# Attention in a fused layer: the exp over three PSUM banks instead of two, and one continuous score pipeline over all head pairs

## The reference

```python
xn = _layernorm(x)
# q, k, v: each holo_linear(xn, basis, phase, amp), split into 16 heads of 64
attn = jnp.einsum('bhqd,bhkd->bhqk', q, k) * scale      # scale = 64 ** -0.5
attn = jax.nn.softmax(attn, axis=-1)
out = jnp.einsum('bhqk,bhkd->bhqd', attn, v)
# out -> holo_linear(..., basis_o, phase_o, amp_o)
x = x + attention(xn) + ffn(xn)                         # ffn: 8 experts + shared MLP
```

## Time and profile before

| what | us |
|---|---|
| runs | 3964.14 and 4123.48, median 4043.81 |
| profiled execution | 3966.25 |
| its span on the slowest core (core 7) | 3964.7 |
| spans of the 8 cores | 3949.5 to 3964.7 |
| first exp of attention starts | 505.5 |
| last exp of attention starts | 1259.5 |
| exps: 512, together busy | 571.8 |

### The profile page before, as it was taken

The page is one execution under the profiler, slowest core; times in us unless marked ns, Lnnn a source line. Parts: engine busy times, 40 slices in busy tenths (PEclk is TensorE's granted clock), DMA queues, the critical chain, the costliest instruction groups (busy, mean ns, idle before and its releaser), DMA issues.

```text
span 3964.7 us, 46389 instructions; the slowest of 8 cores (3949.5 to 3964.7 us)
## 1 busy us (share of the span) xinstructions
PE 3153.2 (80%) x13795; PEld 1235.1 (31%) x13795; DVE 1567.0 (40%) x2502; ACT 939.1 (24%) x1201; POOL 318.1 (8%) x383
## 2 busy tenths in 40 slices
PE   2343356666664489999999999999999999999996
PEld 1111112222221034343343433334434343344432
DVE  4232511111112435444444554544444445433344
ACT  0222167777775011111111100011111110011100
POOL 1111000000000101110000000011000000011000
PEclk9855588888888599999999999999999999999995
DMA  1000000000000143342222222224322222234105
GB/s 30 27 22 22 1 0 1 1 1 1 1 1 11 15 49 36 39 54 33 32 33 32 33 33 32 33 33 54 43 32 33 32 33 33 32 38 56 19 1 160
DMA packets 254442, 116.09 MB, mean 29 GB/s; under 512 B 233592, under 2 KB 233592, under 8 KB 254208
## 3 DMA queue, kind: packets, MB, share of 16 engines
q0 software_dynamic: 245248, 87.87, 19.2%
q1 hardware_dynamic: 8960, 25.24, 2.1%
HBM read 191.40 MB, written 8.39 MB: 50 GB/s over the span
## 4 chain that ended last, share of the span: by engine, by line
PE 70%; ACT 10%; DVE 9%; issue 6%; POOL 2%; DMA 2%; DVEq 1%; ACTq 0%; SPq 0%; POOLq 0%
PE p_xg L821 20%; PE p_xu L830 19%; PE p_d L863 19%; ACT pTs L639 9%; PE p_a L610 3%; PE p_b L610 3%; PE p_sc L629 2%; PE p_t L415 2%; DVE acc L871 1%; DMA out<-o 1%; POOL xnl_tm L407 1%; PE p_pj L295 1%; DVE gbuf L845 1%; DVE acc L722 1%; DVE o_heads L681 1%
## 5 line engine op out<-in xcount | busy, mean ns | idle before, releaser
L863 PE MATMUL p_d<-gbuf,wdbuf 128*128 128x512 bf16 x3520 | 835.4, 378 | 63.8 <-DVE acc L871 34.2
L821 PE MATMUL p_xg<-xnh_fm,wgbuf 128*128 128x512 bf16 x3520 | 844.5, 383 | 25.2 <-DMA wdbuf<-w_down 25.2
L830 PE MATMUL p_xu<-xnh_fm,wubuf 128*128 128x512 bf16 x3520 | 835.3, 380 | 0.0
L840 ACT ACTIVATE sgt<-p_xg 128x512 bf16<-128x512 f32 x440 | 263.2, 598 | 2177.3 <-PE p_xg L821 1535.6
L871 DVE TENSOR_TENSOR acc<-acc,p_d 128x512 f32<-128x512 f32 x896 | 617.0, 689 | 256.9 <-PE p_d L863 242.7
L845 DVE TENSOR_TENSOR gbuf<-sgt,p_xu 128x512 bf16<-128x512 bf16 x440 | 302.6, 688 | 979.6 <-PE p_xu L830 977.4
L639 ACT ACTIVATE pTs<-p_sc,bias 128x1024 bf16<-128x1024 f32 x512 | 571.8, 1117 | 247.6 <-PE p_sc L629 174.4
L821 PEld LDWEIGHTS p_xg<-xnh_fm,wgbuf 128*128 128x128 bf16 x3520 | 346.4, 99 | 449.8 <-issue 42.0
L830 PEld LDWEIGHTS p_xu<-xnh_fm,wubuf 128*128 128x128 bf16 x3520 | 345.7, 98 | 420.3 <-issue 8.8
L863 PEld LDWEIGHTS p_d<-gbuf,wdbuf 128*128 128x128 bf16 x3520 | 285.1, 96 | 609.6 <-issue 390.3
L610 PE MATMUL p_a<-pTs,v_aug 128*65 128x512 bf16 x512 | 175.6, 428 | 238.9 <-ACT pTs L639 214.3
(11 more groups left out here) (200 smaller groups left out, 1001.9 us busy)
## 6 DMA issues: line engine op xcount, KB each, us to landing
wgbuf<-w_gate POOLq DMA_DIRECT2D x88, 256.0 KB, 8.8
wubuf<-w_up POOLq DMA_DIRECT2D x88, 256.0 KB, 9.5
wdbuf<-w_down POOLq DMA_DIRECT2D x88, 256.0 KB, 9.9
x_tm<-x SPq DMA_DIRECT2D x16, 512.0 KB, 4.0
x<-x SPq DMA_DIRECT2D x16, 512.0 KB, 4.3
out<-o SPq DMA_DIRECT2D x16, 512.0 KB, 5.2
wgbuf<-sw_gate POOLq DMA_DIRECT2D x22, 256.0 KB, 7.5
wubuf<-sw_up POOLq DMA_DIRECT2D x22, 256.0 KB, 8.0
```

Source lines behind the costliest of these rows:

```text
L821: emit("tensor", lambda te, buf=buf, loc=loc, c=c, tg=tg, pb=pg_b: te.matmul(pb[:, :], wgbuf[buf][:, loc * 1024 + c * 128: loc * 1024 + c ...
L830: emit("tensor", lambda te, buf=buf, loc=loc, c=c, tg=tg, pb=pu_b: te.matmul(pb[:, :], wubuf[buf][:, loc * 1024 + c * 128: loc * 1024 + c ...
L840: emit("scalar", lambda s, ss=ss, pb=pg_b: s.activation(sgt[ss][:], pb[:, :], AF.Silu), waits=[("t", t_xg), sgt_free[ss]], incs=[("s", 1)])
L863: first=(li == 0), last=(li == len(grp) - 1): te.matmul(pb[:, :], wdbuf[buf][:, li * 1024 + dc * 128: li * 1024 + dc * 128 + 128], gbuf[bu ...
```

## The change

Three things change together.

1. An exp covers three score tiles (1536 columns, three banks) instead of two. `p_sc` is now two halves of three banks (`half_free`) instead of three slots of two banks. Score tiles are counted through the whole stage (`c_ctr`, 1024 of them), exp number e takes tiles 3e to 3e+2, and tile 3e waits for exp e-2. There are 341 exps of 1536 columns and a last one of 512.
2. The loop over blocks and the loop over a block's steps are one loop over 256 steps. Value matmuls are still two steps behind, also across a block's end, and their wait is for the exp that covers the last tile of their step (`chunk_exp`).
3. `pTs` holds 9 tiles instead of 8, as a ring, and the exps no longer wait for the value matmuls. VectorE's copies and SyncE's transfers at a block's end are the same; they are emitted right behind the last value matmuls of the block, ahead of the scores of that step.

```diff
-    pTs = sb("pTs", [128, 4096], BF16, st2)
+    pTs = sb("pTs", [128, 4608], BF16, st2)
...
-    for mi, (hA, hB, qb) in enumerate(pairs):
-        exp_done = [0] * 8
-        for pair in range(10):
-            if pair >= 2:
...
-                            waits=([("s", exp_done[p2])] if (sidx == 0 and j == 0) else []) +
+    nsteps = len(pairs) * 8
+    for s in range(nsteps + 2):
+        if s >= 2:
+            s2 = s - 2
+            mi2, p2 = s2 // 8, s2 % 8
...
+                    rc = 512 * ((4 * s2 + 2 * j + sidx) % 9)
...
+                        waits=([("s", chunk_exp[4 * s2 + 3])]
+                               if (sidx == 0 and j == 0) else []) +
+                              (av_free[sidx] + ([("v", v_vaug_ones)] if mi2 == 0 else [])
+                               if kc == 0 else []),
...
+        if s < nsteps:
+            mi, pair = s // 8, s % 8
+            hA, hB, qb = pairs[mi]
+            for j in (0, 1):
                 for sidx, h in ((0, hA), (1, hB)):
...
+                    half = (c // 3) % 2
+                    coff = half * 1536 + (c % 3) * 512
...
+                        waits=(half_free[half] if c % 3 == 0 else []) +
+                              ([("v", v_bias)] if c == 0 else []),
...
+                    flush = (c % 3 == 2) or (c == nsteps * 4 - 1)
+                    if flush:
+                        e = c // 3
...
-                        waits=[("t", t_sp), pTs_free[pp]], incs=[("s", 1)])
-                    st_ring[r] = [("s", cnt["s"])]
+                             waits=[("t", t_sp)], incs=[("s", 1)])
+                        half_free[half] = [("s", cnt["s"])]
+                        for cc in range(3 * e, c + 1):
+                            chunk_exp[cc] = cnt["s"]
```

More of the change, by code:

```diff
@@ L592, in build_nc @@
     zrow_free = [("dr0", 0), ("dr1", 0)]
-    st_ring = [[("s", s_p1_done), ("v", v_p1_done)] for _ in range(3)]
+    half_free = [[("s", s_p1_done), ("v", v_p1_done)] for _ in range(2)]
     av_free = {0: list(pa_free), 1: list(pbc_free[0])}
-    pTs_free = {0: ("t", 0), 1: ("t", 0)}
-    u_ctr = 0
+    c_ctr = 0
+    chunk_exp = {}
     pairs = [(2 * hp, 2 * hp + 1, qb) for hp in range(NHEAD // 2) for qb in range(NTG)]
-    for mi, (hA, hB, qb) in enumerate(pairs):
-        exp_done = [0] * 8
-        for pair in range(10):
-            if pair >= 2:
-                p2 = pair - 2
-                pp2 = p2 % 2
-                for sidx, h in ((0, hA), (1, hB)):
[L605 to L615, removed]
-                            waits=([("s", exp_done[p2])] if (sidx == 0 and j == 0) else []) +
[L617 to L642, removed]
-                        waits=[("t", t_sp), pTs_free[pp]], incs=[("s", 1)])
-                    st_ring[r] = [("s", cnt["s"])]
[L645 to L664, removed]
@@ L665, in build_nc @@
     dr0_all, dr1_all = cnt["dr0"], cnt["dr1"]
     emit("vector", lambda v: v.reciprocal(p_sc[0:NHEAD, 0:T], zfull[:]),
-         waits=[("dr0", dr0_all), ("dr1", dr1_all)] + st_ring[0] + st_ring[1]
-               + st_ring[2], incs=[("v", 1)])
+         waits=[("dr0", dr0_all), ("dr1", dr1_all)] + half_free[0] + half_free[1],
+         incs=[("v", 1)])
     emit("vector", lambda v: v.tensor_copy(recip16[:], p_sc[0:NHEAD, 0:T]),
```

51 lines of the change are left out of this document (added).

## The result

| what | us |
|---|---|
| before, 10 runs beside those of after | median 3962.97 |
| after, 11 runs | median 4018.08 |
| ratio after/before | 1.0134, 95% interval 1.0095 to 1.0174 |
| after, profiled execution | 4015.77, span 4014.2 (core 5) |
| first exp to end of last exp | 803.8, before 755.1 |

The change makes the kernel 1.3% slower: the sign was forecast, 4136 us and the range from 4030 were too high, and the result lies in the case "within 2%", which had a chance of 0.11. Of the 49.5 us between the two spans 48.7 lie between the first and the last exp, so the stages around attention did not move.

A forecast was written before the change was run, and what follows sets the result against it. ScalarE's exps were taken to bound attention. Exps, own waits, serialised steps and block ends, 558.5 + 69 + 126 + 32 = 786 us, plus 0.62 x 224 for clock, gave stage 925 against 755, time 4136 us; range 4030 to 4190.

The forecast's parts named there:

- within 2%: Outcome case for the whole kernel: a time within about 2%, 79 us, of the kernel before; chance 0.11.
- Step s = 3k+2: Attention: exp 4k+2 waits for exp 4k+1, four value matmuls and one tile; ScalarE idle 1.68 us instead of 0.20.
- 628 us of a ScalarE that is fed without a break: Attention stage from exps (558.5) and own waits (69) alone; rival "faster", time 3839 us, chance 0.03.
- own waits: ScalarE between exps: wait for its own last instruction, 341 by 0.203, 69 us.
- serialised step beyond an own wait: Steps s = 3k+2 at 2.4 GHz: 1.48 us more idle on ScalarE, 85 times, 126 us.
- ends of blocks: Value matmuls on `p_b` wait for VectorE's last copy, ahead of scores ScalarE needs: 1.03, 31 times, 32 us.
- time at 1.2 GHz: Attention stage: added time from TensorE's lower clock, 0.62 x 224 on top of 786 us.
- I take 0.62, midway: Share of the attention stage at the lower clock, between 0.39 to 0.52 and 0.79 or more.
- clock kept: Rival: serialised step present but TensorE keeps 2.4 GHz; stage 786, time 3997 us, chance 0.10.
- the price of 1636 ns: ScalarE: one 1536-column exp, from 598 ns for 512 and 1117 for 1024; exps sum to 558.5 us.
- a higher alternative: Exp of 1536 columns at 1676 ns if cost grows in proportion, 14 us more of the stage.
- I count nothing: ScalarE: dropping the exps' wait on `pTs` was taken to save 0 us.

The follow-up runs named there:

- stage_copy: Changed kernel with VectorE taking all 65 rows of a bank to SBUF in one copy at block ends, freeing the bank with it; ratio 0.9966 to the kernel before.
- slow_exp: stage_copy's kernel with one more ScalarE instruction, a copy of one column, behind every exp; 4061.56 us in the profiled run.
- loop_only: Changed kernel's single loop over 256 steps with the 1024-column exps of before and a pTs ring of 8 tiles; ratio 0.9827 to the kernel before.
- scores_first: Changed kernel with all four score tiles ahead of the value matmuls in every step and a pTs ring of 12 tiles; ratio 0.9788 to the kernel before.
- best: Changed kernel with the edits of scores_first and stage_copy together; ratio 0.9647 to the kernel before.
- loop_stage: Changed kernel with the edits of loop_only and stage_copy together; ratio 0.9736 to the kernel before.

## Why the prediction was wrong

**Right: the mechanism, its place and its sign.** Step s = 3k+2 is serialised, 1.58 us idle measured for 1.68, and moving one tile takes 103 us out of the stage. At 1.2 GHz the same gap measures 2.65 us for the forecast 2.8 (ahead of the exp at 578.66, core 5), and the one two exps later 1.40 for 1.4 (at 572.78). The 628 us of a ScalarE that is fed without a break were indeed out of reach for the order as written.

**Wrong: sizes of the sum.** The forecast stage was 925 us, the measured one 803.8. Term by term, from the gaps of ScalarE on core 5:

| term | forecast | measured | where from |
|---|---|---|---|
| exps | 558.5 | 526.6 | 1542 ns for 1636 |
| own waits | 69 | 50 | 341 by 0.148, for 0.203 |
| serialised step beyond an own wait | 126 | 122 | 85 by 1.43 |
| exp 4k+1 beyond an own wait | 0 | 10 | 86 by 0.11 |
| ends of blocks | 32 | 45 | 31 gaps beyond those of their place |
| time at 1.2 GHz | 139 | 50 | what is left |

What is left is mostly gaps at the lower clock, and it agrees with the price read from the cores: the mean of 0.88 is 186 us at 1.2 GHz, by 0.27 that is 50.

**The step that failed** is "I take 0.62, midway", the share of the stage at 1.2 GHz. It was 0.23 (186 of 803.8 us), and the term measured 50 us instead of 139. I reasoned from one pause, 1.62 us at a block's end, to all pauses of that length. stage_copy has the serialised pauses and a clock of 0.97, and slow_exp has hardly longer ones and 0.82, so the length of these pauses was the wrong quantity. In the earlier trace rows the pause of 1.62 came behind another of 0.93 with four value matmuls between them; in the changed kernel eight matmuls stand between the two long pauses of a cycle and sixteen behind them. The rival "clock kept", 3997 us with 0.10, was closer than my choice, and its stage of 786 would be 754 with the measured terms above. The rule of the Trainium skill cited for it (TensorE: Matmul & The Clock Gate, section HAM oscillation) was nearer for the serialised pauses than I allowed, but the trace does not bear it out: 186 us of the stage are at 1.2 GHz, and no pause of TensorE in it is longer than 1.7 us.

**The second step** is the price of 1636 ns, from rows of two functions: 32 us. The prediction named a higher alternative only; below, and a different slope were open.

**The third** is the own wait. "The dropped wait on `pTs` ended no more than part of 69.0 us [...] I count nothing": the wait between exps fell from 0.203 to 0.148, 19 us over 341 exps, and in loop_only it did so with exps of the old size. A wait that is already met when it is reached ends no idle time in the earlier trace rows, and still seems to have cost 0.055 us each time.

**The fourth** is the ends, too low by 13 us. "I take the row's 1.03, 31 times" used a row that was no wait for the copies: as the two lines from 603.06 show, it was the ordinary wait for an exp. The copies cost ScalarE 0.93 to 2.08 us and more, 1.45 on average. That 32 came near 45 is luck.

## What to carry to other kernels

When an instruction is made to cover more tiles than a step makes, write out for each step which result the consumer in front of the last tile needs; if it is the one just before, the two engines take turns once per cycle. One tile moved ahead decided between 1.3% slower and 1.4% faster here. And where several producers share a queue, look at what happens at the seams (the ends of blocks): early release of the accumulator bank was worth 65 us of the stage in stage_copy, 52 from scores_first to best and 24 from loop_only to loop_stage, the larger instruction 38.

## What the hardware showed

An exp's own wait, from its end to the start of the next one on ScalarE, is 0.203 us in the kernel before and 0.148 in the others but slow_exp, behind exps of 1.114 us (loop_only, loop_stage) as behind those of 1.542. So it is not the exp's length. What the kernels with 0.148 share is one wait less in front of each exp; no run isolates it. The price of the exp is linear in the columns, 264 ns and 0.83 ns for each (from 689, 1117 and 1542). What exactly brings the granted clock down in this stage is open: 0.97 and 0.82 were measured with the same number of waits for an exp ahead of value matmuls, of almost the same length, but with 5 and 114 waits ahead of score tiles.
